# Second biases of the experts: from a matmul with a gathered table to a gather and an add per slot tile; two sets of GpSimd work done at another time

## The reference, cut to what matters

```
h = xf @ shared_w1 + shared_b1
z = swiglu5(h, ...) @ shared_w2 + shared_b2
w, idx = top_k(softmax(xf @ gate_w + gate_b), 2);  w = w / sum(w)
cw = sum(one_hot(idx, 16) * w[..., None], axis=1)
he = einsum('nd,edh->enh', xf, expert_w1) + expert_b1
te = swiglu5(he, ...)
oe = einsum('enh,ehd->end', te, expert_w2) + expert_b2[:, None, :]
y = einsum('ne,end->nd', cw, oe)
return y + z
```

## Time and profile before

| | us |
|---|---|
| median of three runs | 2488.22 |
| the profiled execution | 2485.51 |
| its span, first to last instruction | 2483.8 |
| mixture of experts, from 2100.8 us on | 383 |
| TensorE busy in the span | 2420.4 (97%) |
| VectorE, ScalarE, GpSimd busy | 1389.8, 947.2, 763.3 |

### The profile page before, as it was taken

How to read it: one execution, slowest core, us unless ns; L and a number is a source line. 1 busy time by engine, 2 the same in 40 slices (tenths; PEclk the granted TensorE clock), 3 DMA queues, 4 the chain that set the end, 5 groups by cost and what they waited for, 6 DMA issues and landing times. The chain is left out here.

```text
span 2483.8 us, 27280 instructions
## 1 busy us (share of the span) xinstructions
PE 2420.4 (97%) x9176; PEld 1372.1 (55%) x9176; DVE 1389.8 (56%) x2929; ACT 947.2 (38%) x1615; POOL 763.3 (31%) x1138
## 2 busy tenths in 40 slices
PE   8999999999999999999999999999999999998998
PEld 4565655444676545577555567655467654533343
DVE  7896760522875551687561478643277644633445
ACT  5885642220664210566111266312066522211221
POOL 2005102000654200364210165220056413525564
PEclk9999999999999999999999999999999999999999
DMA  5401001330667210366211166511056611569637
GB/s 163 136 18 37 38 28 36 113 95 1 153 156 190 78 56 0 92 157 162 75 25 38 33 157 159 136 27 39 1 132 156 172 49 44 198 227 337 222 91 231
DMA packets 136804, 264.16 MB, mean 106 GB/s; under 512 B 52499, under 2 KB 52979, under 8 KB 134325
## 3 DMA queue, kind: packets, MB, share of 16 engines
q1 hardware_dynamic: 91655, 159.78, 22.1%
q0 software_dynamic: 43664, 100.31, 15.0%
q10 hardware_dynamic: 1346, 2.33, 0.3%
HBM read 212.80 MB, written 31.93 MB: 99 GB/s over the span
## 5 line engine op out<-in xcount | busy, mean ns | idle before, releaser
L110 POOL DMA_DIRECT2D cols<-w x720 | 352.8, 498 | 850.0 <-DVE w L643 835.0
L439 PE MATMUL psum<-cols,w 128*128 128x500 f32 (+1 forms) x1120 | 393.3, 510 | 1.2 <-PEq L96 1.2
L519 PE MATMUL psum<-cols,rows 128*128 128x256 f32 (+1 forms) x1600 | 371.7, 381 | 8.4 <-DMA cols<-w 8.4
L703 ACT ACTIVATE g_prob<-g_prob,g_row_max 125x1250 f32<-125x1250 f32 x160 | 214.0, 1338 | 412.3 <-DVE g_row_max L630 412.3
L505 PE MATMUL psum<-g_k_cols,g_q_cols 128*125 128x512 f32 (+1 forms) x960 | 361.4, 513 | 3.3 <-DVE g_row_max L627 3.3
L519 PEld LDWEIGHTS psum<-cols,rows 128*128 128x128 f32 (+1 forms) x1600 | 304.7, 191 | 48.6 <-DMA cols<-w 9.8
L439 PEld LDWEIGHTS psum<-cols,w 128*128 128x128 f32 x1120 | 209.9, 189 | 173.0 <-issue 165.0
L627 DVE CUSTOM_DVE_ANT_0 g_prob<-psum,ln_count 125x1250 f32<-125x1250 f32 x160 | 233.6, 1460 | 116.6 <-PE psum L505 116.3
L505 PEld LDWEIGHTS psum<-g_k_cols,g_q_cols 128*125 128x125 f32 x960 | 179.5, 187 | 173.4 <-issue 161.0
L643 DVE STREAM_TRANSPOSE w<-g_prob 128x1280 f32<-128x1280 f32 x160 | 241.1, 1507 | 11.4 <-ACT g_prob L709 11.2
L709 ACT ACTIVATE g_prob<-g_prob,g_row_max 125x1250 f32<-125x1250 f32 x160 | 214.1, 1338 | 57.0 <-DVE g_row_max L617 57.0
(11 more groups left out here) (356 smaller groups left out, 3302.6 us busy)
## 6 DMA issues: line engine op xcount, KB each, us to landing
cols<-w POOLq DMA_DIRECT2D x720, 80.0 KB, 3.3
cols<-w SPq DMA_DIRECT2D x560, 80.0 KB
m_eb<-in_L_ffn_expert_b SPq DMA_DIRECT2D x54, 192.0 KB
w<-in_L_gnn_m_w SPq DMA_DIRECT2D x8, 1024.0 KB
slot_rows<-p_kf SPq DMA_DIRECT2D x1, 7128.0 KB, 32.4
rows<-slot_rows SPq DMA_DIRECT2D x54, 132.0 KB, 4.6
m_ew<-in_L_ffn_expert_w SPq DMA_DIRECT2D x4, 1536.0 KB, 10.7
slot_outputs<-slot_rows SPq DMA_DIRECT2D x1, 5000.0 KB
```

The source lines that it names most:

```text
L110: return eng.dma_start(out, in_, allow_slow_non_contiguous=True)
L439: ins = c.pe.matmul(c.bank(group_bank(g), width), wt[:, k, o * 128:(o + 1) * 128], y_cols[:, k, start:start + width], start=(k == 0), stop ...
L519: ins = pe.matmul(c.bank(6 + g % 2, 256).rearrange("p (u a i) -> p u a i", u=2, a=SIDE), rows[0:r, j, h * 128:(h + 1) * 128], turned_keys[ ...
L703: s.activation(prob[0:P, u, 0:N], prob[0:P, u, 0:N], ACT.Exp, bias=row_max[:, u, 1:2], accum_out=row_max[:, u, 2:3]).then_inc(exp_made, 1)
```

## The change

Three things. (1) `cw`, `cw_cols` and the table `b2` go, with their VectorE, TensorE and DMA work. Instead VectorE makes `bias_of`, an expert number for each partition and pair, past the bound where nothing has to be loaded (every partition but the first of the tile pair, when the expert is that of the turn before). GpSimd gathers rows of the second biases with it into a ring of three tiles `eb2`, for pairs 0 to 2 before its loop, for pair i + 3 behind pair i's store. VectorE adds the bias to the output from PSUM (`out_dve(i)`, behind `glu_dve(i + 1)` in its order), and ScalarE then scales in SBUF. (2) GpSimd's sums of the store places are made once ahead of its loop, from `place_in`, which SyncE loads with six loads of column D of `slot_rows`, each 64 partitions x 9 numbers of 4 bytes, between stream 3's weights and the wait for the shared expert's down products. (3) At the end, VectorE adds GpSimd's sums first: four tiles of them before the first product with the slot matrix, then always four tiles ahead.

```diff
@@ -2192,6 +2194,8 @@
...
         expert_f, same, weights_f = (x_flat[:, S * (EXPERTS + n):S * (EXPERTS + n + 1)] for n in range(3))
+        bias_f = x_flat[:, 1280:1280 + PAIRS].rearrange("p (q s) -> p s q", s=SIDES)
+        by_stream = lambda v, e: v[e * HALF:(e + 1) * HALF].rearrange("p (s e q) -> p e s q", s=SIDES, e=2)[:, e]
         turned_logit = x_all[0:EXPERTS].rearrange("p u c n -> p (u c n)")[:, 0:N]
@@ -2244,7 +2249,6 @@
...
                     b1_in, 16)
-            load(sp, b2[:], a["L0_ffn_expert_b2"]).then_inc(w2_in, 16)
             load(sp, w2, chunks(a["L0_ffn_shared_w2"])).then_inc(w2_in, 16)
@@ -2444,31 +2448,13 @@
...
             v.tensor_copy(weights_of[:], weights_f[:]).then_inc(weights_of_made, 1)
-            for k in range(2):
-                v.tensor_tensor(pick[:, k], pick[:, k], over_experts(weight[:, :, k]), ALU.mult).then_inc(step, 1)
-            v.wait_ge(step, n + 2)
-            v.tensor_tensor(cw[:], pick[:, 0], pick[:, 1], ALU.add).then_inc(cw_made, 1)
-        CW_PARTS = [(0, 4), (4, 8), (8, NT)]
-        def cw_pe(i):
-            pe = c.pe
-            pe.wait_ge(cw_made, 1)
-            if i == 2:
-                pe.wait_ge(cw_cols_made, 1)
-            for t in range(*CW_PARTS[i]):
-                at = (6 + i % 2) * BANK + t % 4 * P
-                ins = pe.transpose(psum[0:EXPERTS, at:at + P], cw[:, t, :], ident[0:P, 0:P])
-            ins.then_inc(cw_turned, 1)
-        def cw_dve(i):
-            t0, t1 = CW_PARTS[i]
-            c.dve.wait_ge(cw_turned, i + 1)
-            c.dve.tensor_copy(cw_cols[:, t0 * P:t1 * P], c.bank(6 + i % 2, (t1 - t0) * P, EXPERTS)).then_inc(
-                cw_cols_made, 1)
-        CW_AFTER = {4: 0, 5: 1, 6: 2}
+            for e in range(2):
+                v.scalar_tensor_tensor(bias_f[lanes(e)][:, :, 1:], by_stream(same, e)[:, :, 1:], lane_of[lanes(e), 1:2],
+                                       by_stream(expert_f, e)[:, :, 1:], ALU.mult, ALU.add).then_inc(step, 1)
+                v.tensor_copy(bias_f[lanes(e)][:, :, 0:1], by_stream(expert_f, e)[:, :, 0:1]).then_inc(step, 1)
+            v.wait_ge(step, n + 4)
+            v.tensor_copy(bias_of[:].rearrange("p (q s) -> p s q", s=SIDES), bias_f).then_inc(bias_of_made, 1)
@@ -2521,23 +2505,18 @@
...
                                        ALU.mult).then_inc(h_made, 1)
-                if n in CW_AFTER:
-                    cw_dve(CW_AFTER[n])
         def shared_down_pe():
             pe = c.pe
             pe.wait_ge(h_made, len(GROUPS))
-            pe.wait_ge(w2_in, 32)
-            pe.wait_ge(cw_cols_made, 3)
+            pe.wait_ge(w2_in, 16)
             for t in range(NT):
...
                 for k in range(IC):
-                    pe.matmul(c.bank(t % 4, D, P), hidden[:, k, t * P:(t + 1) * P], w2[:, k, :], start=(k == 0),
-                              stop=False)
-                pe.matmul(c.bank(t % 4, D, P), cw_cols[:, t * P:(t + 1) * P], b2[:, :], start=False,
-                          stop=True).then_inc(s_mm, 1)
+                    ins = pe.matmul(c.bank(t % 4, D, P), hidden[:, k, t * P:(t + 1) * P], w2[:, k, :], start=(k == 0),
+                                    stop=(k == IC - 1))
+                ins.then_inc(s_mm, 1)
@@ -2574,7 +2553,6 @@
...
                 sp.wait_ge(out_made, i - R + 1)
-                sp.wait_ge(place_made, 2 * (i - R) + 1)
             for e, s in enumerate(streams(i)):
@@ -2591,6 +2569,10 @@
...
             load_first_weights(3)
+            for e in range(2):
+                for i in range(SIDES):
+                    load(sp, place_in[lanes(e), i::SIDES], slot_dram[:, :].rearrange("(s p) d -> p s d", p=HALF)[
+                        :, tile_of(2 * i + e, 0):tile_of(2 * i + e + 1, 0), D]).then_inc(blank_in, 16)
             sp.wait_ge(s_mm, NT)
@@ -2682,7 +2664,7 @@
...
                 if i >= 1:
-                    pe.wait_ge(out_made, i)
+                    pe.wait_ge(out_biased, i)
                 for s in streams(i):
@@ -2734,6 +2715,13 @@
...
+        def out_dve(i):
+            v = c.dve
+            u = i % U
+            v.wait_ge(down_mm, i + 1)
+            v.wait_ge(out_bias_in[u], 16 * rounds(i))
+            v.tensor_tensor(h[u][:, 0:D], c.bank(OUT), eb2[u][:, :], ALU.add).then_inc(out_biased, 1)
         def take_x(i):
@@ -2766,8 +2754,8 @@
...
                     sigmoid(i + 1)
-                s.wait_ge(down_mm, i + 1)
-                s.activation(h[u][:, 0:D], c.bank(OUT), ACT.Identity, scale=rows[:, i % R, D + 1:D + 2]).then_inc(out_made, 1)
+                s.wait_ge(out_biased, i + 1)
+                s.activation(h[u][:, 0:D], h[u][:, 0:D], ACT.Identity, scale=rows[:, i % R, D + 1:D + 2]).then_inc(out_made, 1)
@@ -2781,13 +2769,22 @@
...
+            def out_biases(i):
+                g.indirect_dma_start(
+                    out=eb2[i % U][:, :], out_offset=None, in_=a["L0_ffn_expert_b2"],
+                    in_offset=bass.IndirectOffsetOnAxis(ap=bias_of[:, i:i + 1], axis=0),
+                    bounds_check=EXPERTS - 1, oob_is_err=False).then_inc(out_bias_in[i % U], 16)
+            g.wait_ge(bias_of_made, 1)
+            for i in range(U):
+                out_biases(i)
+            g.wait_ge(blank_in, 16 * STREAMS)
+            g.tensor_tensor(blank_place[:], place_in[:], blank_place[:], ALU.add).then_inc(place_made, 1)
+            g.wait_ge(place_made, 1)
+            g.tensor_copy(slot_place[:], blank_place[:]).then_inc(place_made, 1)
             g.wait_ge(weights_of_made, 1)
+            g.wait_ge(place_made, 2)
             for i in range(PAIRS):
-                g.wait_ge(slot_in[i % R], 32 * (i // R + 1))
-                g.tensor_tensor(blank_place[:, i:i + 1], rows[:, i % R, D:D + 1], blank_place[:, i:i + 1], ALU.add).then_inc(
-                    place_made, 1)
-                g.wait_ge(place_made, 2 * i + 1)
-                g.tensor_copy(slot_place[:, i:i + 1], blank_place[:, i:i + 1]).then_inc(place_made, 1)
                 if turn(i) + 1 < TURNS:
@@ -2795,11 +2792,12 @@
...
                     continue
-                g.wait_ge(place_made, 2 * i + 2)
                 g.wait_ge(out_made, i + 1)
...
                     out_offset=bass.IndirectOffsetOnAxis(ap=slot_place[:, i:i + 1], axis=0)).then_inc(stored[i % U], 16)
+                if i + U < PAIRS:
+                    out_biases(i + U)
@@ -2813,7 +2811,7 @@
...
             for t in range(NT):
-                sp.wait_ge(summed, t + 1)
+                sp.wait_ge(hot_added, t + 1)
                 load_tile(sp, out[t * P:(t + 1) * P, :], x[:, t, :], out_stored)
@@ -2825,12 +2823,19 @@
...
             v = c.dve
+            def add_back(t):
+                v.wait_ge(added, t + 1)
+                v.tensor_tensor(x[:, t, :], x[:, t, :], back[t][:, 0, :], ALU.add).then_inc(summed, 1)
+            for t in range(BACK_EARLY):
+                add_back(t)
             for t in range(NT):
+                if t + BACK_EARLY < NT:
+                    add_back(t + BACK_EARLY)
+                v.wait_ge(summed, t + 1)
                 v.wait_ge(hot_mm, t + 1)
                 v.tensor_tensor(x[:, t, :], x[:, t, :], c.bank(HOT_BANKS[t], D, P), ALU.add).then_inc(hot_added, 1)
-                v.wait_ge(hot_added, t + 1)
-                v.wait_ge(added, t + 1)
-                v.tensor_tensor(x[:, t, :], x[:, t, :], back[t][:, 0, :], ALU.add).then_inc(summed, 1)
@@ -2858,6 +2863,9 @@
...
                 glu_dve(i)
+                if i >= 1:
+                    out_dve(i - 1)
+            out_dve(PAIRS - 1)
             combine_dve()
```

More of the change, by code:

```diff
@@ L2124, in moe @@
                                                                    "r_expert_made", "r_pos_made")
-    places_made, scattered, cw_made, cw_turned, cw_cols_made = c.sems("r_places_made", "r_scattered", "r_cw_made",
-                                                                      "r_cw_turned", "r_cw_cols_made")
+    places_made, scattered, bias_of_made, blank_in = c.sems("r_places_made", "r_scattered", "r_bias_of_made",
+                                                            "e_place_in")
+    out_bias_in = [c.sem(f"e_out_bias_in{u}") for u in range(U)]
+    out_biased = c.sem("e_out_biased")
     b2_added, h_mm, biased, clipped, sig_made, glu_step, h_made = c.sems(
@@ L2155, in moe @@
         t_all = sb("m_t_cols", [128, U, IC, 128])
-        cw = sb("m_cw", [P, NT, EXPERTS])
-        cw_cols = sb("m_cw_cols", [EXPERTS, N])
-        b2 = sb("m_b2", [EXPERTS, D])
+        eb2 = ring("m_eb2_", [128, D])
         shared_b2 = sb("m_shared_b2", [P, D])
@@ L2185, in moe @@
         blank_place = sb("m_blank_place", [128, PAIRS])
+        place_in = sb("m_place_in", [128, PAIRS])
+        bias_of = sb("m_bias_of", [128, PAIRS], U32)
         prm = sb("m_prm", [EXPERTS + 1, 8])
@@ L2224, in moe @@
         shifted = [w_free[:, P + (1 + n) * NT:P + (2 + n) * NT] for n in range(2)]
+        BACK_EARLY = 4
         HOT_BANKS = [2, 3, 4, 5, 0, 1, TURN, OUT, 2, 3]
```

3 lines of the change are left out of this document (removed).

## The result

| | us | against before |
|---|---|---|
| before, median of 4 runs beside it | 2488.64 (2487.75 to 2493.63) | |
| changed kernel, median of 4 runs | 2505.26 (2504.24 to 2506.25) | 1.0063, 95% interval 1.0045 to 1.008 |
| changed kernel, profiled execution | 2504.24 | |
| predicted | 2492.2 (2484.0 to 2500.0) | |

The account below looks back on a forecast made before the run. TensorE was taken to bound the last stage only where no weight is late. Start -2.0, middle +5.0 and end +1.0 us sum to +4.0 on the 2488.22 us median: 2492.2 us, range 2484 to 2500.

Parts of the forecast that it names:

- Part 1: Shared expert's down products: without bias products and transposes TensorE ends 11.6 us earlier, and so pair 0 starts earlier.
- Part 2: Start of expert stage: stream 3's weights don't move, so TensorE idles until 2202.1 us before pair 1, then restarts at half clock.
- a way of being wrong: Start of expert stage: the prediction is wrong if the scatters, and with them SyncE's row loads, shift.
- Part 3: Six element-wise loads before pair 2: issue covered, 3 us on DMA engines; of 11.6 us saved, 2.0 are left.
- the second (small loads that hold the engines): Rival at the start: 3456 separate pieces at 60 ns each cost 13 us on the DMA engines, giving 2502 us; 15%.
- Part 4: GpSimd's loop: bias gather and later store issue each weight gather 1.0 us later, costing 2 x 1.0 us in the stall.
- Part 5: Saturated stretch: 0.85 MB of bias rows cost 2.6 us, skipped rows 0.4 us; with the gathers' later issue, +5.0 us.
- The third rival: Waits before pairs grow long enough for the lower clock, 3.1 us each; two give 2498.5 us; 12%.
- Part 6: End: the hop delays the last products, and the first back sums stand behind pair 26's bias addition; +1.0 us.
- The fourth rival: Expert loop: the output's hop over VectorE exceeds ScalarE's 0.9 us slack, 0.3 us in each of 25 rounds, 2499.7 us; 5%.

Follow-up runs that it names:

- a_skip_gather: Changed kernel with all 24 second-bias gathers inside the loop issued, but every index past the bound, so they write nothing; ratio 1.0032, 2496.7 us.
- the four relatives of the kernel before: Kernel before with place loads and sums (1.0006), new last-sum order (0.9988), that plus early stream 3 weights (0.9996), or place loads, reordered SyncE, new last sums (1.0001).
- b_combine: The kernel before with only the new order of the last sums; ratio 0.9988 (0.9977 to 1.0).

## Why the prediction was wrong, point by point

- **Part 1** held: pair 0 starts 11.7 us sooner; 11.6 were forecast.
- **Part 2** held in its mechanism: stream 3's weights were the next thing late, landed 7.1 us after their issue, and TensorE stood idle until 2202.29 us (2202.1 forecast) and came back at a clock of 0.50. That the two times agree is in part luck: counted from the stage's start TensorE came back 2.5 us late, after 8.74 us of idle time, because SyncE's row loads had shifted, which the prediction named as a way of being wrong.
- **Part 3** is the step that failed. It looked for the price on the DMA engines and took SyncE's issue as 6 x 0.47 us, covered by the wait for the shared products. The issue took 8.95 us and bound: stream 4's weights went out 9.1 us later than the forecast had them, some 6 of it by the issue's length and 2.6 by the row loads ahead. Pair 2 came 6.1 us later than before instead of 2.0 sooner, an error of 8 us. The Trainium skill, page "DMA: Bandwidth & Descriptors", section "Rules for kernel authors", warns of one descriptor per element, and the traces agree that such loads are dear: 13.8 KB held SyncE for 8.95 us. The price per packet, the page's 10.5 ns as well as my 9 ns from the earlier trace rows, fits what the pieces took of the DMA engines, 8.8 ns each, and says nothing of SyncE. No run shows SyncE's time for a load as proportional to pieces alone, since the same six take 4.0 to 16.7 us. Of the rivals, the second (small loads that hold the engines) had the right size, 2502 us, by the wrong resource: it wanted 30 to 60 ns a piece.
- **Part 4** held and was worth less than said. The store ends at 2260.82 us and the weight gather starts at 2262.46, the 1.64 us of the forecast:

```profile
2259.78 1.04 POOL L2796 DMA_INDIRECT slot_outputs<-m_work,m_slot_place  x1 [0.30 <-issue]
2261.13 1.03 POOL L2773 DMA_INDIRECT m_eb<-in_L_ffn_expert_b,m_bias_of  x1 [0.30 <-issue]
2262.46 1.00 POOL L2767 DMA_INDIRECT w<-in_L_ffn_expert_w,m_weights_of  x1 [0.30 <-issue]
```

  But `a_skip_gather`, which has those instructions, costs no more than the run without them.
- **Part 5** had the mechanism and was too small, though by how much is unsure. It counted 0.85 MB and 2.6 us. The 1.60 MB and 4.9 us measured are those of the whole loop; from 2205 to 2353 us, when the last stall ends, 26.93 MB passed on GpSimd's queue, 12 stores of 0.26 MB among them. At 2.36 MB of weights and 0.13 MB of bias rows a change of expert, these are an estimated 9 to 10 changes, 1.2 MB of bias rows and 3.8 us. Stalls grew by 7.9 us. The third rival (half-clock restarts, 3.1 us for each) was also real: two restarts more than before in the middle. What one costs there I can read only as products of 1.09 us instead of 0.61. The middle, from pair 2 to pair 14, took 11.6 us longer where +5.0 stood; against the four relatives of the kernel before (125.4 to 127.9 us, with 134.0 in the changed kernel) it is 6 to 9 us.
- **Part 6** had the last sum's end right, 30.7 us after pair 26's step against 30.9 measured, and missed 1.9 us of stores behind it. It said in so many words that the back sums stood behind the bias addition, not in VectorE's idle time; `b_combine` shows that this, not the new order, is what costs: without the hop the last part is up to 2.7 us shorter, with it 3.0 us longer. Its sum is 17.5 us by its own terms, not 17.6, which changes nothing.
- **The fourth rival**, that the hop costs more, is where the end belongs: it was sized for the loop, where its cost is within the intervals.

Against the forecast the start is worse by 8.1 us, the middle by 6.6 and the end by 2.0, 16.7 in all. With the 4.0 forecast and 0.3 between pair 14 and 26 that is 21.0 us, from 383.0 to 404.0. This is the difference of two single traces, and the quick middle of the one before makes up an estimated 3 to 5.5 us of it. The start is the surest of the three: without its 8.1 us the changed kernel's median would lie inside the range.

## What to carry to other kernels

Price a moved load first by the queue that issues it: here six element-wise loads held their issuing engine for 4 to 17 us, longer the more data stood in front of them on the queue, and everything behind them waited. When work is taken off the engine that bounds the stage, look at once at the next thing due in each queue; here 11.6 us off TensorE were worth nothing until SyncE's order was changed too. And in a stretch in which the DMA engines are full, price a replacement by what it moves: 1.6 MB of repeated bias rows cost some 7 of the 11.6 us that the removed products gave. Last, compare a stage with several traces of near relatives before calling a few us a finding.

## What the runs showed of the hardware that I had not expected

- SyncE's issue of the same six loads (3456 pieces of 4 bytes) took 4.04 to 4.72 us with only row loads just ahead of them (four kernels), 8.04 to 8.96 us behind 2.3 MB of weights (seven kernels), and 16.70 us behind 6.9 MB. The issue grew with what was queued ahead, and the pieces passed only when that was through; two small loads of m_b took 0.93 us.
- A gather whose rows are all past the bound still sends as many packets (17744 in both kernels, 15824 without the 24 gathers) and holds GpSimd for 1.02 us, but its time could not be told from no gather at all.
